# Surface flow: the sum of p2 and q2 as an addition on GpSimd over 128x1024 elements instead of an accumulating DMA

## The chip, the cores and the metric

The kernel runs on one core of a Trainium2 chip. The metric is the device time of one execution in microseconds (us); lower is better. The engines of the core are named as in the profile: PE (TensorE, matmuls), DVE (VectorE), ACT (ScalarE), POOL (GpSimd) and SP (SyncE, which here only issues DMAs). The engines run side by side and meet through semaphores.

## The reference

Four layers in a row over images of shape (4, 16, 512, 512) in fp32: window attention with an MLP, a surface flow of ten time steps, and two residual pairs of 3x3 convolutions. Only the flow matters here:

```python
def step(u, _):
    ux, uy, uxx, uxy, uyy = _derivs(u)          # Sobel 3x3, clipped to +-10
    g2 = ux * ux + uy * uy
    denK = jnp.maximum(1.0 + g2, EPS)
    K = jnp.clip((uxx * uyy - uxy * uxy) / (denK * denK + EPS), -5.0, 5.0)
    denH = jnp.sqrt(1.0 + g2 + EPS)
    H = ((1.0 + uy * uy) * uxx - 2.0 * ux * uy * uxy + (1.0 + ux * ux) * uyy) / (2.0 * denH ** 3 + EPS)
    H = jnp.clip(H, -5.0, 5.0)
    diff = jnp.clip(alpha * K + beta * H, -1.0, 1.0)
    u = u + DT * diff
    u = jnp.pad(u[:, :, 1:-1, 1:-1], ((0, 0), (0, 0), (1, 1), (1, 1)), mode='edge')
    return (u, None)
u, _ = jax.lax.scan(step, x, None, length=TIME_STEPS)      # 10 steps
return 0.7 * u + 0.3 * x
```

The change is about `g2 = ux*ux + uy*uy`, in the kernel's names q2 = p2 + q2.

## The kernel before, in words

The kernel has three stages one after the other: `attention_stage`, `surface_stage` (the flow) and `conv_chain` (both convolution layers). Only `surface_stage` is touched.

It takes the 64 images in 8 groups of 8. A group lies in SBUF as the tensor u with 17 units, each 128 partitions by two images' rows of 512 (128x1024 elements). It goes through its ten time steps there, so there are 8 x 10 x 17 = 1360 units in all. Between two steps SP exchanges halo rows between units by small DMAs, and between two groups it stores u and loads the next group (`boundary`).

Each engine runs a loop of slots written out by hand, and slot n does the work of several units of different age:

- PE (L872) makes five derivatives of unit n in PSUM, in the order B, p, A, q, C, by fp32 matmuls with band matrices: p = ux, q = uy, A, B, C the second derivatives.
- ACT copies them out of PSUM (L895 p, L899 A, L901 q, L909 B, L921 C), squares the clipped p and q together into p2q2 (L929), which is the tile p2 beside the tile q2, and makes the denominators of unit n-2 out of the sum in q2: rK at L913, L915 and L926, rH at L917, L924 and L936, and L904 one slot later. B2 is the square of B (L933).
- DVE clips (L1009 A, L1016 p and q, L1034 C, L1041 B) and makes the products: Ha = (q2 + 1) A (L1038, which reads q2 before the sum overwrites it), nK = -A C (L1027), m = m B (L1031), nK = nK rK of unit n-2 (L1048), rH = beta Hc rH of unit n-2 (L1051), Hc = (p2 + 1) C (L1060), m = -2 p q (L1064), ds (L1021, clipped at L1044), and the edge columns of u (L1056).
- POOL computes nothing. It issues accumulating DMAs (destination = destination + source, SBUF to SBUF) for all sums: nK += B2 (L956, unit n-1), q2 += p2 (L962, unit n), u += ds (L969, three DMAs for unit n-3), Hc += m (L975, unit n-1) and Hc += Ha (L981, unit n).

Every engine takes its instructions in their order, so what stands behind a waiting instruction waits with it. Every tile except u is there twice, by the parity of the unit. `g_sum` is the semaphore of the sum in q2: ACT waits for it ahead of L913, two slots after POOL issues the sum, and POOL waits ahead of L962 for the sum of the unit before. `t1_done` is set by DVE's L1038 and `squared["pq"]` by ACT's L929; POOL waits for both ahead of the sum.

Of the kernel before, what the change touches and what calls it, by code (L numbers as in the profile page):

```python
# [11 lines left out]
ALU = mybir.AluOpType  # L12
# [589 lines left out]
def surface_stage(nc, x1, u10, mats, alpha_in, beta_in, STEPS):  # L602
# [45 lines left out]
    with ExitStack() as ctx:  # L648
# [3 lines left out]
        def sem(name):  # L652
            return ctx.enter_context(nc.semaphore(name))
# [14 lines left out]
        for i, n in enumerate("pq"):  # L668
# [10 lines left out]
        g_sum, ac_done, numk, pq_done, t12_done, numh, u_added = (  # L679
            sem(n) for n in ("g_sum", "ac_done", "numk", "pq_done", "t12_done", "numh", "u_added"))  # L680
        den_squared, den_ln, g_ln, g_pow, pow_ln, rk_done, rh_done = (
            sem(n) for n in ("den_squared", "den_ln", "g_ln", "g_pow", "pow_ln", "rk_done", "rh_done"))
        sums_begun, taps_begun = sem("sums_begun"), sem("taps_begun")
# [4 lines left out]
        def here(unit):  # L688

            return not isinstance(unit, int) or 0 <= unit < TOTAL  # L690

        def wait(eng, s, value):

            if not isinstance(value, int) or value > 0:
                eng.wait_ge(s, value)


        def flat(ap):
            return ap.rearrange("p t w -> p (t w)")

        def buf(n, par):
            return flat(bufs[n][:, par])

        def both(pair, par):

            return pair[:, par].rearrange("p n t w -> p (n t w)")

        def bank(name):

            return banks["pABqC".index(name) % 4]  # L710
# [173 lines left out]
        @block.scalar  # L884
        def _(act):

            act.preload_act_table_set("natural_log_exp_and_others")

            def slot(n, par):

                o = 1 - par
                if here(n):
                    act.wait_ge(made["p"], n + 1)
                    wait(act, pq_done, n - 1)
                    act.activation(buf("pc", par), flat(bank("p")[:, :, :]), ACT.Copy).then_inc(copied["p"], 1)  # L895
                    act.wait_ge(made["A"], n + 1)
                    wait(act, t1_done, n - 1)
                    wait(act, ac_done, n - 1)
                    act.activation(buf("Ac", par), flat(bank("A")[:, :, :]), ACT.Copy).then_inc(copied["A"], 1)  # L899
                    act.wait_ge(made["q"], n + 1)  # L900
                    act.activation(buf("qc", par), flat(bank("q")[:, :, :]), ACT.Copy).then_inc(copied["q"], 1)  # L901
                if here(n - 3):
                    act.wait_ge(pow_ln, n - 2)
                    act.activation(buf("rH", o), buf("rH", o), ACT.Exp, scale=-1.0).then_inc(rh_done, 1)  # L904
                if here(n):
                    act.wait_ge(made["B"], n + 1)
                    wait(act, m_done, n - 1)
                    wait(act, squared["B"], n - 1)
                    act.activation(buf("Bc", par), flat(bank("B")[:, :, :]), ACT.Copy).then_inc(copied["B"], 1)  # L909
                if here(n - 2):  # L910
                    act.wait_ge(g_sum, (n - 1) * 16)
                    wait(act, k_made, n - 3)
                    act.activation(buf("rK", par), buf("q2", par), ACT.Square, bias=1.0).then_inc(den_squared, 1)  # L913
                    act.wait_ge(den_squared, n - 1)
                    act.activation(buf("rK", par), buf("rK", par), ACT.Ln, bias=EPS).then_inc(den_ln, 1)  # L915
                    wait(act, s_done, n - 3)
                    act.activation(buf("rH", par), buf("q2", par), ACT.Ln, bias=1.0 + EPS).then_inc(g_ln, 1)  # L917
                if here(n):
                    act.wait_ge(made["C"], n + 1)
                    wait(act, t2_done, n - 1)  # L920
                    act.activation(buf("Cc", par), flat(bank("C")[:, :, :]), ACT.Copy).then_inc(copied["C"], 1)  # L921
                if here(n - 2):
                    act.wait_ge(g_ln, n - 1)
                    act.activation(buf("rH", par), buf("rH", par), ACT.Exp, scale=1.5).then_inc(g_pow, 1)  # L924
                    act.wait_ge(den_ln, n - 1)
                    act.activation(buf("rK", par), buf("rK", par), ACT.Exp, scale=-1.0).then_inc(rk_done, 1)  # L926
                if here(n):
                    act.wait_ge(clipped["pq"], n + 1)
                    act.activation(both(p2q2, par), both(pq, par), ACT.Square).then_inc(squared["pq"], 1)  # L929
                if here(n - 1):  # L930
                    act.wait_ge(clipped["B"], n)
                    wait(act, k_made, n - 2)
                    act.activation(buf("B2", o), buf("Bc", o), ACT.Square).then_inc(squared["B"], 1)  # L933
                if here(n - 2):
                    act.wait_ge(g_pow, n - 1)
                    act.activation(buf("rH", par), buf("rH", par), ACT.Ln, bias=EPS, scale=2.0).then_inc(pow_ln, 1)  # L936

            for n in range(4):
                slot(n, n % 2)
            with act.Fori(4, TOTAL - 2, 2) as n:  # L940
                slot(n, 0)
                slot(n + 1, 1)
            for n in range(TOTAL - 2, TOTAL + 3):
                slot(n, n % 2)

        @block.gpsimd
        def _(pool):
            def slot(n, par):

                o = 1 - par  # L950
                if here(n - 1):
                    pool.wait_ge(ac_done, n)
                    pool.wait_ge(squared["B"], n)
                    wait(pool, numk, (n - 1) * 16)
                    pool.sem_inc(sums_begun, 1)
                    pool.dma_start(buf("nK", o), buf("B2", o), accum_op=ALU.add).then_inc(numk, 16)  # L956
                if here(n):
                    pool.wait_ge(squared["pq"], n + 1)
                    pool.wait_ge(t1_done, n + 1)
                    wait(pool, g_sum, n * 16)  # L960
                    pool.sem_inc(sums_begun, 1)
                    pool.dma_start(buf("q2", par), buf("p2", par), accum_op=ALU.add).then_inc(g_sum, 16)  # L962
                if here(n - 3):
                    pool.wait_ge(s_clipped, n - 2)
                    wait(pool, u_added, (n - 3) * 48)
                    pool.sem_inc(sums_begun, 1)
                    k, ds = bass.ds((n - 3) % UNITS, 1), bufs["ds"][:, o]
                    for t, rows, found in HALVES:
                        pool.dma_start(u[rows, k, t, 2:W + 2].rearrange("p a w -> p (a w)"), ds[found, t, :], accum_op=ALU.add).then_inc(u_added, 16)  # L969
                if here(n - 1):  # L970
                    pool.wait_ge(t12_done, n * 16)
                    pool.wait_ge(m_done, n)
                    wait(pool, numh, (n - 1) * 16)
                    pool.sem_inc(sums_begun, 1)
                    pool.dma_start(buf("Hc", o), buf("m", o), accum_op=ALU.add).then_inc(numh, 16)  # L975
                if here(n):
                    pool.wait_ge(t1_done, n + 1)
                    pool.wait_ge(t2_done, n + 1)
                    wait(pool, t12_done, n * 16)
                    pool.sem_inc(sums_begun, 1)  # L980
                    pool.dma_start(buf("Hc", par), buf("Ha", par), accum_op=ALU.add).then_inc(t12_done, 16)  # L981

            for n in range(4):
                slot(n, n % 2)
            with pool.Fori(4, TOTAL - 2, 2) as n:
                slot(n, 0)
                slot(n + 1, 1)
            for n in range(TOTAL - 2, TOTAL + 3):
                slot(n, n % 2)
# [441 lines left out]
```

## Time and profile before

| | |
|---|---|
| time, median of 2 runs | 28,650.49 us (28,632.75 to 28,668.22) |
| the profiled execution | 28,647.74 us, its span 28,645.9 us |
| PE busy | 26,744.7 us, 93% |
| DVE busy | 23,740.9 us, 83% |
| ACT busy | 23,103.3 us, 81% |
| POOL busy | 8,975.8 us, 31% |
| TensorE's granted clock, mean | 0.981 |

The span is the time from the first to the last instruction of the profiled execution. The shares are means over three stages with different limits, so they have to be read stage by stage. In the rows below, a row of waits names the engine and instruction that stood still, what released it, the time in all, how often, and the longest. A row of a group has the line, engine and operation, the tiles (out<-in) with their shapes and the count, then busy time and mean duration, then the idle time just before them. "Landing" is the time from the issue of a DMA to its completion.

### The profile page before, as it was taken

How to read it: one execution, taken by the hardware profiler on the slowest of the kernel's cores; microseconds unless marked ns; L12 is line 12 of the kernel's file. 1: busy time of each engine (PE TensorE's matmuls, PEld its weight loads, DVE VectorE, ACT ScalarE, POOL GpSimd, SP SyncE). 2: the span in 40 equal slices, each digit the busy share in tenths (PEclk: the TensorE clock that was granted, in tenths of full speed). 3: DMA queues.
4: the chain of work that ended last, by engine and by line, in shares of the span. 5: the costliest groups of instructions: out<-in, count | busy, mean ns of one | idle time of the engine just before them, and what ended most of it. 6: DMA issues, size and time to landing. Idle time of an engine off the chain costs nothing. (4 is left out here: it accounts for less than half of the span.)

```text
span 28645.9 us, 827717 instructions
## 1 busy us (share of the span) xinstructions
PE 26744.7 (93%) x334232; PEld 12655.2 (44%) x334232; DVE 23740.9 (83%) x26151; ACT 23103.3 (81%) x23277; POOL 8975.8 (31%) x9524
## 2 busy tenths in 40 slices
PE   8999999999989989998999899999989998999799
PEld 5666666444334433443434344334434443444455
DVE  6666666799989989998999899889989998999222
ACT  6666666799989989998999899889989998999111
POOL 0000000244434434443444344434434443444000
PEclk9999999999999999999999999999999999999899
DMA  1111111699999999999999999999999999999654
GB/s 33 32 32 32 32 32 32 126 176 176 178 177 176 177 177 178 176 176 178 176 176 178 178 176 176 180 175 176 176 178 175 176 176 179 176 176 176 119 106 90
DMA packets 1942097, 4147.74 MB, mean 145 GB/s; under 512 B 590960, under 2 KB 722544, under 8 KB 1938160
## 3 DMA queue, kind: packets, MB, share of 16 engines
q0 software_dynamic: 1196800, 3565.77, 70.6%
q1 hardware_dynamic: 701424, 469.69, 8.2%
q10 hardware_dynamic: 41088, 67.14, 1.1%
q8 instruction: 2726, 44.66, 0.6%
q14 instruction: 59, 0.48, 0.0%
HBM read 294.41 MB, written 201.33 MB: 17 GB/s over the span
## 5 line engine op out<-in xcount | busy, mean ns | idle before, releaser
L872 PE MATMUL surf_ps<-surf_u,surf_matf 64*64 64x512 f32 x184960 | 20141.9, 593 | 1129.8 <-ACT surf_pq L895 703.1
L872 PEld LDWEIGHTS surf_ps<-surf_u,surf_matf 64*64 64x64 f32 x184960 | 8316.3, 133 | 12956.2 <-issue 12897.1
L929 ACT ACTIVATE surf_p2q<-surf_pq 128x2048 f32<-128x2048 f32 x1360 | 2599.9, 1912 | 1484.5 <-DVE surf_pq L1016 1484.5
L969 POOL DMA_DIRECT2D surf_u<-surf_ds x4080 | 3458.4, 1156 | 954.0 <-issue 483.3
L962 POOL DMA_DIRECT2D surf_p2q<-surf_p2q x1360 | 1161.3, 854 | 7773.6 <-DVE surf_Ha L1038 7280.0
L956 POOL DMA_DIRECT2D surf_nK<-surf_B x1360 | 1236.4, 909 | 6884.4 <-ACT surf_B L933 6870.3
L1051 DVE SCALAR_TENSOR_TENSOR surf_rH<-surf_Hc,surf_dt_ab,surf_rH 128x1024 f32<-128x1024 f32 x1360 | 1744.0, 1282 | 1454.7 <-DMA surf_Hc<-surf_m 1045.0
L981 POOL DMA_DIRECT2D surf_Hc<-surf_Ha x1360 | 2187.1, 1608 | 351.2 <-DVE surf_Hc L1060 344.2
L975 POOL DMA_DIRECT2D surf_Hc<-surf_m x1360 | 1466.2, 1078 | 1648.1 <-DMA surf_Hc<-surf_Ha 1521.8
L1027 DVE SCALAR_TENSOR_TENSOR surf_nK<-surf_Ac,surf_Cc 128x1024 f32<-128x1024 f32 x1360 | 1666.8, 1226 | 180.6
L1021 DVE SCALAR_TENSOR_TENSOR surf_ds<-surf_nK,surf_dt_ab,surf_rH 128x1024 f32<-128x1024 f32 x1360 | 1731.0, 1273 | 0.3
L1060 DVE SCALAR_TENSOR_TENSOR surf_Hc<-surf_p2q,surf_Cc 128x1024 f32<-128x1024 f32 x1360 | 1666.6, 1225 | 24.0
L404 ACT ACTIVATE att_hid<-att_w,att_b_fc 128x2048 f32<-128x2048 f32 x256 | 503.7, 1968 | 1464.9 <-PE att_w L275 1464.9
L1038 DVE SCALAR_TENSOR_TENSOR surf_Ha<-surf_p2q,surf_Ac 128x1024 f32<-128x1024 f32 x1360 | 1656.0, 1218 | 5.2 <-ACT surf_p2q L929 5.2
L1016 DVE TENSOR_SCALAR surf_pq<-surf_pq 128x2048 f32<-128x2048 f32 x1360 | 1651.9, 1215 | 6.2 <-ACT surf_pq L901 6.2
L1031 DVE TENSOR_TENSOR surf_m<-surf_m,surf_Bc 128x1024 f32<-128x1024 f32 x1360 | 1656.8, 1218 | 0.0
L1064 DVE SCALAR_TENSOR_TENSOR surf_m<-surf_pq 128x1024 f32<-128x1024 f32 x1360 | 1656.7, 1218 | 0.0
L1048 DVE TENSOR_TENSOR surf_nK<-surf_nK,surf_rK 128x1024 f32<-128x1024 f32 x1360 | 1655.2, 1217 | 1.3 <-DMA surf_nK<-surf_B 1.3
L895 ACT ACTIVATE surf_pq<-surf_ps 128x1024 f32<-128x1024 f32 x1360 | 1363.6, 1003 | 331.6 <-PE surf_ps L872 331.6
L483 DVE TENSOR_REDUCE att_mx<-att_w 128x32 f32<-128x2048 f32 x512 | 1173.3, 2292 | 520.8 <-PE att_w L204 520.8
L469 DVE SCALAR_TENSOR_TENSOR att_acc<-att_xin,att_vec,att_acc 128x512 f32<-128x512 f32 x2048 | 1535.1, 750 | 54.3
L901 ACT ACTIVATE surf_pq<-surf_ps 128x1024 f32<-128x1024 f32 x1360 | 1391.3, 1023 | 116.2 <-PE surf_ps L872 98.2
(107 smaller groups left out, 39009.4 us busy)
## 6 DMA issues: line engine op xcount, KB each, us to landing
surf_p2q<-surf_p2q POOLq DMA_DIRECT2D x1360, 512.0 KB, 11.3
surf_Hc<-surf_Ha POOLq DMA_DIRECT2D x1360, 512.0 KB, 13.4
surf_nK<-surf_B POOLq DMA_DIRECT2D x1360, 512.0 KB, 9.6
surf_Hc<-surf_m POOLq DMA_DIRECT2D x1360, 512.0 KB, 11.5
surf_u<-surf_ds POOLq DMA_DIRECT2D x1360, 256.0 KB, 5.7
surf_u<-surf_ds POOLq DMA_DIRECT2D x2720, 128.0 KB, 9.6
att_xin<-in_x SPq DMA_DIRECT2D x2048, 41.2 KB, 2.1
attended<-att_out_rows SPq DMA_DIRECT2D x1024, 64.0 KB, 2.0
```

The source lines that it names most:

```text
L872: mm = pe.matmul(ps[out, t, :], matf[rows, mat, :], u[rows, k, t, off + 2:off + 2 + W], start=(i == 0), stop=(i == len(taps) - 1))
L929: act.activation(both(p2q2, par), both(pq, par), ACT.Square).then_inc(squared["pq"], 1)
L969: pool.dma_start(u[rows, k, t, 2:W + 2].rearrange("p a w -> p (a w)"), ds[found, t, :], accum_op=ALU.add).then_inc(u_added, 16)
L981: pool.dma_start(buf("Hc", par), buf("Ha", par), accum_op=ALU.add).then_inc(t12_done, 16)
L1021: dve.scalar_tensor_tensor(out=buf("ds", o), in0=buf("nK", o), scalar=minus_alpha, in1=buf("rH", o), op0=ALU.mult, op1=ALU.add).then_inc(s ...
L1027: dve.scalar_tensor_tensor(out=buf("nK", o), in0=buf("Ac", o), scalar=-1.0, in1=buf("Cc", o), op0=ALU.mult, op1=ALU.mult).then_inc(ac_done, 1)
L1031: dve.tensor_tensor(buf("m", o), buf("m", o), buf("Bc", o), ALU.mult).then_inc(m_done, 1)
L1038: dve.scalar_tensor_tensor(out=buf("Ha", par), in0=buf("q2", par), scalar=1.0, in1=buf("Ac", par), op0=ALU.add, op1=ALU.mult).then_inc(t1_ ...
L1048: dve.tensor_tensor(buf("nK", par), buf("nK", par), buf("rK", par), ALU.mult).then_inc(k_made, 1)
L1051: dve.scalar_tensor_tensor(out=buf("rH", par), in0=buf("Hc", par), scalar=beta, in1=buf("rH", par), op0=ALU.mult, op1=ALU.mult).then_inc(h ...
L1060: dve.scalar_tensor_tensor(out=buf("Hc", par), in0=buf("p2", par), scalar=1.0, in1=buf("Cc", par), op0=ALU.add, op1=ALU.mult).then_inc(t2_ ...
L1064: dve.scalar_tensor_tensor(out=buf("m", par), in0=buf("pc", par), scalar=-2.0, in1=buf("qc", par), op0=ALU.mult, op1=ALU.mult).then_inc(pq ...
```

## The change

The sum q2 = p2 + q2 of each unit is made by GpSimd itself, as an elementwise addition of two 128x1024 fp32 tiles in SBUF, in the place in POOL's order where it issued the accumulating DMA. POOL's wait on `g_sum` for the sum before and the count `sums_begun` go with the DMA, and ACT's wait on `g_sum` counts by 1 instead of 16. Nothing else changes; the tiles, the other four sums and all other waits stay.

```diff
                 if here(n - 2):
-                    act.wait_ge(g_sum, (n - 1) * 16)
+                    act.wait_ge(g_sum, n - 1)
                     wait(act, k_made, n - 3)
                     act.activation(buf("rK", par), buf("q2", par), ACT.Square, bias=1.0).then_inc(den_squared, 1)
...
                 if here(n):
                     pool.wait_ge(squared["pq"], n + 1)
                     pool.wait_ge(t1_done, n + 1)
-                    wait(pool, g_sum, n * 16)
-                    pool.sem_inc(sums_begun, 1)
-                    pool.dma_start(buf("q2", par), buf("p2", par), accum_op=ALU.add).then_inc(g_sum, 16)
+                    pool.tensor_tensor(buf("q2", par), buf("p2", par), buf("q2", par), ALU.add).then_inc(g_sum, 1)
```

This is POOL's order in the loop of the flow, at the sum of the first of the two slots that the loop holds, with what each row waits for; - is before and + is after the change.

```order
 L695 ISA [waits squared_B,ac_done]
 L956 DMA surf_nK<-surf_B 128x1024 [waits numk]
 L958 REGISTER_ALU
-L695 REGISTER_ALU [waits t1_done,squared_pq]
-L962 DMA surf_p2q<-surf_p2q 128x1024 [waits g_sum]
-L964 REGISTER_ALU
+L960 TENSOR_TENSOR surf_p2q<-surf_p2q 128x1024 [waits t1_done,squared_pq]
+L962 REGISTER_ALU
 L695 ISA [waits s_clipped]
```

The addition stands where the DMA stood, between the sum into nK and the three sums into u; nothing passes anything else. The lines behind it move up by two in the changed kernel (L1038 is L1036 there).

## Rows read from the trace of the kernel before

**Rows 1.** The page, parts 1 and 2: busy time, then tenths in 40 slices.
```profile
PE 26744.7 (93%) x334232; PEld 12655.2 (44%) x334232; DVE 23740.9 (83%) x26151; ACT 23103.3 (81%) x23277; POOL 8975.8 (31%) x9524
...
PE   8999999999989989998999899999989998999799
...
DVE  6666666799989989998999899889989998999222
ACT  6666666799989989998999899889989998999111
POOL 0000000244434434443444344434434443444000
PEclk9999999999999999999999999999999999999899
DMA  1111111699999999999999999999999999999654
```

**Rows 2.** Busy time of each engine in the surface flow; columns in the first line.
```profile
core 0: us, PE busy (x) PEld busy (x) DVE busy (x) ACT busy (x) POOL busy (x), PEclk, DMA share, GB/s
5290.00:26510.00 21220.00, 20113.73 (x184724) 8305.82 (x184720) 19562.92 (x21701) 19235.42 (x19001) 8948.48 (x9493) 0.98 0.98 177
```

**Rows 3.** DMA queues and issues in 6000 to 7000 us: packets, MB, share; KB, landing.
```profile
q0 software_dynamic: 57838, 172.63, 97.7%
...
surf_Hc<-surf_Ha POOLq DMA_DIRECT2D x66, 512.0 KB, 13.3
surf_nK<-surf_B POOLq DMA_DIRECT2D x66, 512.0 KB, 9.5
surf_p2q<-surf_p2q POOLq DMA_DIRECT2D x66, 512.0 KB, 10.6
surf_Hc<-surf_m POOLq DMA_DIRECT2D x66, 512.0 KB, 11.5
surf_u<-surf_ds POOLq DMA_DIRECT2D x66, 256.0 KB, 5.7
surf_u<-surf_ds POOLq DMA_DIRECT2D x132, 128.0 KB, 8.7
```

**Rows 4.** Waits in the surface flow: total us, times, longest.
```profile
ACT surf_p2q L929 <- DVE surf_pq L1016: 1475.0, 1353, 6.2
DVE surf_rH L1051 <- DMA surf_Hc<-surf_m: 1021.4, 495, 11.2
PE surf_ps L872 <- ACT surf_pq L895: 700.8, 418, 5.5
...
DVE surf_rH L1051 <- ACT surf_rH L904: 400.0, 63, 38.2
PE surf_ps L872 <- SPq L841: 368.1, 14, 41.5
...
POOL surf_p2q L962 <- DMA surf_p2q<-surf_p2q: 7.3, 4, 2.0
```

**Rows 5.** Instructions on p2q: ns min/median/max; who waited; landing of the DMA.
```profile
L1038 DVE SCALAR_TENSOR_TENSOR surf_Ha<-surf_p2q,surf_Ac x1360: 1212/1218/1227, 5295.1 to 26540.2; 128x1024 f32<-128x1024 f32 x195
...
L962 POOL DMA_DIRECT2D surf_p2q<-surf_p2q x1360: 850/852/1114, 5297.0 to 26542.0; - x195
...
  ACT surf_rK L913: 8.2, 1
...
DMA to landing us min/median/max: 4.7/11.3/19.1
```

**Rows 6.** The timeline of POOL at the start: its only computing.
```profile
0.25 0.10 POOL L1425 MEMSET const-float32-0.0<- 128x1 f32 x1 [0.25 <-issue]
```

**Rows 7.** The timeline of one slot around L962: start us, us, engine, line.
```profile
12990.66 1.22 DVE L1038 SCALAR_TENSOR_TENSOR surf_Ha<-surf_p2q,surf_Ac 128x1024 f32<-128x1024 f32 x1
...
12991.79 0.69 DVE L1041 TENSOR_SCALAR surf_Bc<-surf_Bc 128x1024 f32<-128x1024 f32 x1
...
12992.40 0.69 DVE L1044 TENSOR_SCALAR surf_ds<-surf_ds 128x1024 f32<-128x1024 f32 x1
...
12992.60 0.85 POOL L962 DMA_DIRECT2D surf_p2q<-surf_p2q  x1 [1.67 <-DVE surf_Ha L1038]
...
12993.00 1.22 DVE L1048 TENSOR_TENSOR surf_nK<-surf_nK,surf_rK 128x1024 f32<-128x1024 f32 x1
...
12994.24 1.29 DVE L1051 SCALAR_TENSOR_TENSOR surf_rH<-surf_Hc,surf_dt_ab,surf_rH 128x1024 f32<-128x1024 f32 x1
```

**Rows 8.** Groups of DVE in the surface flow: busy us, mean ns of one.
```profile
L1031 DVE TENSOR_TENSOR surf_m<-surf_m,surf_Bc 128x1024 f32<-128x1024 f32 x1357 | 1653.1, 1218 | 0.0
...
L1016 DVE TENSOR_SCALAR surf_pq<-surf_pq 128x2048 f32<-128x2048 f32 x1358 | 1649.5, 1215 | 6.2 <-ACT surf_pq L901 6.2
...
L1041 DVE TENSOR_SCALAR surf_Bc<-surf_Bc 128x1024 f32<-128x1024 f32 x1358 | 930.9, 685 | 0.0
```

**Rows 9.** Busy time of each engine around a group boundary, columns as in 2.
```profile
7700.00:8100.00 400.00, 317.17 (x2828) 124.69 (x2824) 300.04 (x334) 295.26 (x292) 141.97 (x146) 0.91 0.93 178
```

## Prediction

> **What bounds the kernel now.** I read the page from the slices down. [rows 1] show three stages: attention to slice 7, the surface flow to slice 37, the convolution chain behind it. Only the flow has GpSimd at work and the DMA engines at 9 tenths; the change is in it alone. It runs from 5290 to 26510 us of the span, 21,220 us for 1360 slots (one unit each), so 15.60 us a slot. The rest, 28,647.7 - 21,220 = 7,428 us, is not touched.
>
> Next the busy times of that stretch [rows 2]: PE 20,114, DVE 19,563, ACT 19,235 and POOL 8,948 us of 21,220; per slot 14.79, 14.38, 14.14 and 6.6 us. Three engines lie within 5% of each other, and the DMA engines are at 0.98 too. Which of them sets the pace is read from the quiet stretch of 1000 us with 66 slots [rows 3]: POOL's queue alone takes 97.7% of 16 engines, 14.8 us a slot. It moves four sums of 512 KB and 512 KB in three parts into u, 2,560 KB a slot. So the DMA engines are the fullest, by a nose.
>
> The waits [rows 4] show how that reaches the others. DVE waits 1,021 us in all at L1051 for the landed sum Hc<-m, in 495 of 1360 slots; ACT in turn waits 1,475 us at L929 for DVE's clip of pq, and PE 701 us for ACT to copy p out of PSUM (L895). PE further waits 368 us for SyncE at L841 (14 times, up to 41.5 us: group boundaries), and DVE 400 us behind ACT L904 at the same places. So DMA -> DVE -> ACT -> PE is the chain of a slow slot, and its head is DVE's wait for DMA.
>
> **The change part by part.**
>
> *The DMA that goes.* 1360 accumulating DMAs of 512 KB each leave POOL's queue: a fifth of 2,560 KB, so 14.8 us a slot becomes about 11.8 us and the DMA engines stop being the bound. The other sums land sooner, and I take DVE's whole wait for them away: -1,021 us of DVE idle time. Its other idle time, 21,220 - 19,563 - 1,021 = 636 us (400 of it at the boundaries), I keep.
>
> *POOL's own time.* The DMA's issue, 0.85 us [rows 5], becomes an addition. POOL is busy 6.6 us a slot, so some 1.3 to 3 us more fits easily in 14 to 17. Behind the addition stand, in POOL's order, the three DMAs into u, Hc<-m, Hc<-Ha and the next nK<-B2. They are issued later by the length of the addition less 0.85 us, but each then finds a queue that is a fifth emptier; I set both at nothing. If that cover is gone, DVE's 1,021 us come back at L1051 and are the price.
>
> *The latency of the sum.* It took 11.3 us to land at the median and 19.1 at most [rows 5]. Its readers (ACT L913 and L917) come two slots, some 31 us, later, and ACT's wait there was 8.2 us once [rows 5]. A sooner sum is worth nothing. The waits on g_sum that go from POOL held it 7.3 us in all [rows 4]: nothing.
>
> *What the addition costs DVE.* This is the term that decides. Before, no row has GpSimd computing on anything but 128x1 constants [rows 6], so it must be bounded. DVE's instructions stand back to back [rows 7]: each starts up to 0.09 us before the one ahead ends, with no free place of a microsecond in the slot. Where GpSimd's addition starts (released by L1038, in the row of the DMA 0.7 us behind its end), DVE is in L1044 and has L1048 and L1051 next. Let x be what DVE loses per addition; the stage is then 19,563 + 636 + 1360x = 20,199 + 1360x, as long as that exceeds PE's floor below.
> - From below x is 0. DVE's L1038 takes 1212 to 1227 ns in all 1360 cases [rows 5], so GpSimd's descriptor work beside it does nothing to it; if an addition is as harmless, DVE loses nothing.
> - From above the nearest thing is the shortest landing of the same sum as a DMA, 4.7 us [rows 5].
> - Between them stand DVE's own rows [rows 8]. A clip of 2048 elements takes 1215 ns and one of 1024 elements 685: 530 ns for 1024 elements and 155 fixed. The two-operand product of 1024 elements (L1031) takes 1218, of which 1063 is streaming. An adder that fetches its operands one after the other streams twice 1063 = 2.13 us.
>
> I take x = 2.13, which is a choice: that GpSimd needs two passes, and that DVE, nearly all of whose instructions move whole tiles in and out of SBUF, stands for that time. No row shows either. It gives 20,199 + 2,897 = 23,096 us, 1,876 more than now. The one-pass row (x = 1.22) would give 21,858, +638; three passes, with the write (x = 3.19), 24,537, +3,317; x = 4.7 26,591, +5,371.
>
> The Trainium skill speaks to just this and against the change. "SBUF — State Buffer", section Who interferes with whom, says that GpSimd reads and writes through a port pair shared with VectorE, and that an instruction of either holds it to its end while the other stands still; it counts VectorE's two-operand instructions and its fast one-operand ones among the holders. "GPSIMD Engine Reference", section 3.1, has 4497 ns for such an addition of 2048 fp32 elements; half of it, an estimate of 2.25 us, would make the stage 23,259 and the run 30,687 us. No run here shows either yet.
>
> **The sum.** 28,648 (the profiled run, 2.7 us under the median of the runs shown) - 1,021 + 2,897 = 30,524 us, +6.5%. PE then has 17.0 us for 14.8 us of work. Its clock stays, I think: at the boundary stretch, with PE busy 317 of 400 us, the granted clock was still 0.91 [rows 9], while at 23,096 us PE would be busy 87%; even at 0.91 against 0.98 its 14.8 us become 15.9, under 17.0.
>
> **The rivals.**
> 1. *The addition is free for DVE (x below about 0.3).* For it: L1038's constant duration. Against it: it rests on descriptor work, not on an operation that reads operands of 512 KB. Then PE sets the pace: 20,114 of work and its other idle time, 1,106 - 701 = 405, make 20,519 us, and the run 27,947, -2.4%. If only some of PE's 701 us goes (ACT is at 14.14 us a slot, and the slots need not be even) it is 28,100 to 28,300, within 2%.
> 2. *A part of it is hidden (x from 0.3 to 1.17).* DVE breaks even at x = 1,021/1360 = 0.75 us, and is 2% slower (573 us) at 1.17. For it: DVE's remaining idle time of 0.47 us a slot can take some. Against it: that time is bunched at boundaries, and even one pass of DVE's own speed is above 1.17. About 28,650.
> 3. *GpSimd waits for DVE instead.* Since DVE has hardly a gap, the addition may begin only where DVE stops. Then Hc<-m behind it is issued late, and DVE's next idle time is L1051 itself, for the addition and then a landing of 11.5 us [rows 3]: some 14 us a slot at worst, or anything between. Against it: a boundary between two instructions of DVE comes every 1.3 us at the latest [rows 7]. From 32,000 up, and 2.5 us of such waiting a slot is where it would pass the likeliest case.
>
> **How the numbers follow.** Likeliest, 0.70: DVE stands for one to three passes, 29,286 (28,648 + 638) to 31,965 us, and 30,524 at two. Rival 1: 0.18, of which 0.12 below -2% and 0.06 within. Rival 2: 0.08, within 2%. Rival 3: 0.04, slower. So faster 0.12, within 2% (about what a measurement of this kernel can tell from no change) 0.14, slower 0.74. The range goes from 28,050, which leaves out the faster case (0.12), to 31,970, which leaves out rival 3: 0.16 left out. The likeliest case's own range is 29,290 to 31,970.
>
> **What would show it.** Right: POOL rows of the addition near 2.1 to 2.3 us; DVE rows behind L1038 (L1044, L1048 or L1051 by the old numbers) longer by about its length, or a gap before them; DVE's share of the flow near all of it, its wait for Hc<-m gone or small; DMA share of the flow near 0.72; PE's wait for L895's copy grown to about 2 us a slot. Wrong, if DVE's busy time in the flow stays at 19,563 us and PE's at the front (rival 1), or if the addition's row is preceded by long idle time and DVE waits longer for Hc<-m than now (rival 3). The step I trust least is x.

## The result, and the profile after

| | before | after |
|---|---|---|
| time, median | 28,650.49 us | 30,076.41 us (30,062.19 to 30,090.63) |
| ratio, 95% interval | | 1.0501 (1.0482 to 1.0519) |
| span of the profiled execution | 28,645.9 us | 30,060.4 us |
| DVE busy | 23,740.9 us | 26,642.0 us |
| PE busy | 26,744.7 us | 26,783.1 us |
| POOL busy | 8,975.8 us | 11,256.3 us |
| granted clock | 0.981 | 0.993 |

The changed kernel is 5% slower, 1,426 us. The line numbers behind the change are lower by two: L1042, L1046, L1049 and L1058 were L1044, L1048, L1051 and L1060.

The slices of the page show the exchange; they answer to [rows 1].

```profile
PE   8999999888888888888888888888888888888799
...
DVE  6666666999999999999999999999999999999422
...
PEclk9999999999999999999999999999999999999899
DMA  1111111677777787778777777777787777777654
```

DVE has gone from 9 tenths with dips to 9 in every slice of the flow, the DMA engines from 9 to 7 or 8 tenths. The busy times of the flow, from the same start to where the changed one ends, answer to [rows 2]:

```profile
core 0: us, PE busy (x) PEld busy (x) DVE busy (x) ACT busy (x) POOL busy (x), PEclk, DMA share, GB/s
5290.00:27930.00 22640.00, 20145.20 (x184552) 8215.77 (x184548) 22437.80 (x21679) 19190.99 (x18979) 11213.06 (x9481) 1.00 0.73 134
```

DVE is busy 22,438 of 22,640 us, so 202 us idle where it was 1,657. The DMA share fell from 0.98 to 0.73. The queues and issues of 1000 quiet us, now with 60 slots in them, answer to [rows 3] (packets, MB and share of 16 engines; then KB and the median time to landing):

```profile
q0 software_dynamic: 44096, 125.59, 69.5%
...
surf_Hc<-surf_m POOLq DMA_DIRECT2D x60, 512.0 KB, 6.2
surf_Hc<-surf_Ha POOLq DMA_DIRECT2D x60, 512.0 KB, 7.9
```

The sum Hc<-m lands after 6.2 us instead of 11.5. The waits of the flow, in all us, times and longest, answer to [rows 4]:

```profile
ACT surf_p2q L929 <- DVE surf_pq L1014: 3375.8, 1354, 3.0
PE surf_ps L872 <- ACT surf_pq L895: 2466.4, 1335, 2.3
...
DVE surf_rH L1049 <- ACT surf_rH L904: 6.0, 5, 2.4
...
DVE surf_rH L1049 <- DMA surf_Hc<-surf_m: 0.3, 1, 0.3
```

DVE's wait for the landed sum, 1,021 us before, is 0.3 us. ACT's wait for DVE has more than doubled (1,475 before) and PE's for ACT has grown from 701 to 2,466 us: the chain is now DVE -> ACT -> PE, and DVE waits for next to nothing. Where its time goes is in the timeline of one slot, answering to [rows 7] (start us, duration us):

```profile
12992.85 1.22 DVE L1036 SCALAR_TENSOR_TENSOR surf_Ha<-surf_p2q,surf_Ac 128x1024 f32<-128x1024 f32 x1
...
12993.99 0.69 DVE L1039 TENSOR_SCALAR surf_Bc<-surf_Bc 128x1024 f32<-128x1024 f32 x1
...
12994.23 2.67 POOL L960 TENSOR_TENSOR surf_p2q<-surf_p2q 128x1024 f32<-128x1024 f32 x1 [1.17 <-DVE surf_Ha L1036]
...
12994.59 2.85 DVE L1042 TENSOR_SCALAR surf_ds<-surf_ds 128x1024 f32<-128x1024 f32 x1
...
12997.37 1.21 DVE L1046 TENSOR_TENSOR surf_nK<-surf_nK,surf_rK 128x1024 f32<-128x1024 f32 x1
...
12998.27 1.72 POOL L967 DMA_DIRECT2D surf_u<-surf_ds  x2 [1.37 <-DVE surf_ds L1042]
```

GpSimd starts its addition at 12994.23, while DVE's clip L1039 runs. That clip ends on time. The next one, L1042, is 0.69 us of work and takes 2.85: it ends 0.54 us after the addition. The addition ends at 12996.90. The groups of DVE in the flow show that this holds for the mean of all slots (busy us, mean ns of one), answering to [rows 8]:

```profile
L1042 DVE TENSOR_SCALAR surf_ds<-surf_ds 128x1024 f32<-128x1024 f32 x1353 | 3876.3, 2865 | 0.0
...
L1029 DVE TENSOR_TENSOR surf_m<-surf_m,surf_Bc 128x1024 f32<-128x1024 f32 x1355 | 1650.5, 1218 | 0.0
...
L1039 DVE TENSOR_SCALAR surf_Bc<-surf_Bc 128x1024 f32<-128x1024 f32 x1356 | 928.8, 685 | 0.0
```

The clip of ds takes 2,865 ns in the mean. In [rows 7] it was 0.69 us, and its twin L1039 still is 685. The others kept their length to within 20 ns; only the small operation on the edge columns of u, L1054, went from 182 to 229 ns. The shortest, median and longest duration of the instructions on p2q, answering to [rows 5], show that the loss isn't bound to the clip:

```profile
L1036 DVE SCALAR_TENSOR_TENSOR surf_Ha<-surf_p2q,surf_Ac x1360: 1214/1217/1226, 5297.5 to 27981.9; 128x1024 f32<-128x1024 f32 x195
L960 POOL TENSOR_TENSOR surf_p2q<-surf_p2q x1360: 2372/2672/2689, 5298.9 to 27983.2; 128x1024 f32<-128x1024 f32 x195
L1058 DVE SCALAR_TENSOR_TENSOR surf_Hc<-surf_p2q,surf_Cc x1360: 1224/1225/4080, 5299.2 to 27988.9; 128x1024 f32<-128x1024 f32 x195
```

L1036, ahead of the addition, is untouched in all 1360 cases. The Hc product L1058, an instruction with two operands, reached 4,080 ns: in the first slots no unit n-3 exists, L1042 is not there to be hit, and L1058 (twice) and L1046 (once) were hit in its place.

### The profile page after: what moved, and what is told of

Its sections match the earlier page's. It is cut to its first block and busy times, and to the rows that moved or that the text cites. A ratio compares the mean times of both kernels' runs of the same rounds, so it can differ in the third digit from the quotient of the medians.

```text
span 30060.4 us, 825006 instructions
## 1 busy us (share of the span) xinstructions
PE 26783.1 (89%) x334232; PEld 12568.7 (42%) x334232; DVE 26642.0 (89%) x26151; ACT 23081.5 (77%) x23277; POOL 11256.3 (37%) x9524
## 5 line engine op out<-in xcount | busy, mean ns | idle before, releaser
L960 POOL TENSOR_TENSOR surf_p2q<-surf_p2q 128x1024 f32<-128x1024 f32 x1360 | 3627.2, 2667 | 6815.5 <-DVE surf_Ha L1036 6815.2
L1042 DVE TENSOR_SCALAR surf_ds<-surf_ds 128x1024 f32<-128x1024 f32 x1360 | 3889.8, 2860 | 0.1
L973 POOL DMA_DIRECT2D surf_Hc<-surf_m x1360 | 2158.9, 1587 | 15.9 <-DMA surf_Hc<-surf_Ha 4.0
L979 POOL DMA_DIRECT2D surf_Hc<-surf_Ha x1360 | 1785.2, 1313 | 12.5 <-issue 7.6
L1049 DVE SCALAR_TENSOR_TENSOR surf_rH<-surf_Hc,surf_dt_ab,surf_rH 128x1024 f32<-128x1024 f32 x1360 | 1730.1, 1272 | 13.2 <-DMA surf_Hc<-surf_m 7.2
L1058 DVE SCALAR_TENSOR_TENSOR surf_Hc<-surf_p2q,surf_Cc 128x1024 f32<-128x1024 f32 x1360 | 1671.4, 1229 | 1.4
L1036 DVE SCALAR_TENSOR_TENSOR surf_Ha<-surf_p2q,surf_Ac 128x1024 f32<-128x1024 f32 x1360 | 1655.6, 1217 | 5.2 <-ACT surf_p2q L929 5.2
L1029 DVE TENSOR_TENSOR surf_m<-surf_m,surf_Bc 128x1024 f32<-128x1024 f32 x1360 | 1656.6, 1218 | 0.0
L1062 DVE SCALAR_TENSOR_TENSOR surf_m<-surf_pq 128x1024 f32<-128x1024 f32 x1360 | 1656.5, 1218 | 0.0
L1046 DVE TENSOR_TENSOR surf_nK<-surf_nK,surf_rK 128x1024 f32<-128x1024 f32 x1360 | 1649.9, 1213 | 5.4 <-DMA surf_nK<-surf_B 5.4
L915 ACT ACTIVATE surf_rK<-surf_rK 128x1024 f32<-128x1024 f32 x1360 | 1438.5, 1058 | 43.2
```

The source lines that it names most:

```text
L960: pool.tensor_tensor(buf("q2", par), buf("p2", par), buf("q2", par), ALU.add).then_inc(g_sum, 1)
L1029: dve.tensor_tensor(buf("m", o), buf("m", o), buf("Bc", o), ALU.mult).then_inc(m_done, 1)
L1042: dve.tensor_scalar(buf("ds", o), buf("ds", o), DT, -DT, ALU.min, ALU.max).then_inc(s_clipped, 1)
L1049: dve.scalar_tensor_tensor(out=buf("rH", par), in0=buf("Hc", par), scalar=beta, in1=buf("rH", par), op0=ALU.mult, op1=ALU.mult).then_inc(h ...
L1058: dve.scalar_tensor_tensor(out=buf("Hc", par), in0=buf("p2", par), scalar=1.0, in1=buf("Cc", par), op0=ALU.add, op1=ALU.mult).then_inc(t2_ ...
```

## Experiments

Theory S: GpSimd's addition stands DVE still for as long as it streams its operands, and that is all of the loss. Rivals: the loss comes from POOL's order (O), from both costs adding (A), or from something that depends on the place of the addition.

### What the DMA's removal is worth alone

```diff
-                    pool.tensor_tensor(buf("q2", par), buf("p2", par), buf("q2", par), ALU.add).then_inc(g_sum, 1)
+                    pool.sem_inc(g_sum, 1)
```

> Leaves the sum out: neither a DMA nor an addition, so q2 keeps the square of q. It measures what the removed DMA is worth alone. Theory S (GpSimd's addition stands DVE still, 2.17 us a slot, and nothing else costs): DVE's wait of 1021 us for the landed Hc<-m is gone and PE sets the pace, 27,950 us, or 27,600 if the boundary waits of 368 us go as well. Rival O (the loss comes from POOL's order, from issues that come at another time without the DMA): no better than before, 28,650 or above.

Measured: 27,518.0 us, 0.9610 of before (0.9594 to 0.9626). Rival O in its first form falls: POOL's order without the DMA costs nothing. What a long instruction in that order costs, by the later issues behind it, this run does not test; the changed kernel's waits show it, with DVE 0.3 us behind Hc<-m. The quiet 1000 us show the new leader (columns as above):

```profile
6000.00:7000.00 1000.00, 1000.00 (x9324) 505.39 (x9320) 988.67 (x1096) 977.94 (x960) 385.10 (x410) 1.00 0.81 147
```

PE is busy all of it at 9324 matmuls, at 136 a slot 14.59 us a slot. I had expected 27,950, or 27,600 with the boundary waits gone. They are not quite gone: PE still waited 214 us for SP at the boundaries. Against this kernel, and not against the one before, the addition on GpSimd costs 30,076 - 27,518 = 2,558 us, 1.88 us a slot. So the removal brought 1,120 us (28,638 in the same session less 27,518) and the addition took 2,558.

### The addition on DVE itself

```diff
                     dve.tensor_scalar(buf("Bc", par), buf("Bc", par), *CLIP).then_inc(clipped["B"], 1)
+                    dve.wait_ge(t1_done, n + 1)
+                    dve.tensor_tensor(buf("q2", par), buf("p2", par), buf("q2", par), ALU.add).then_inc(g_sum, 1)
...
-                    pool.tensor_tensor(buf("q2", par), buf("p2", par), buf("q2", par), ALU.add).then_inc(g_sum, 1)
```

> The same addition on DVE, behind its clip of B, with no DMA and nothing on POOL. Theory S: it costs DVE its own 1.13 us (1.22 less the overlap with its neighbours) instead of 2.17, so 1,040 ns x 1360 = 1,410 us less than with GpSimd: about 28,650 us, the time of the kernel before. Rival O (the loss comes through POOL's longer queue, later sums into u and Hc): the same gain over the GpSimd version, but DVE idle and not 99% busy. Rival T (DVE stands still whenever its two-operand work meets POOL's descriptor work): slower than 28,900.

Measured: 28,746.3 us, 1.0040 (1.0026 to 1.0054): 0.4% slower than before, about 100 us more than expected, and 1,330 us faster than with the addition on GpSimd. The groups of DVE in the flow:

```profile
L1037 DVE TENSOR_TENSOR surf_p2q<-surf_p2q 128x1024 f32<-128x1024 f32 x1360 | 1660.0, 1221 | 0.0
...
L1040 DVE TENSOR_SCALAR surf_ds<-surf_ds 128x1024 f32<-128x1024 f32 x1360 | 936.9, 689 | 0.1
```

The addition takes DVE 1,221 ns, and the clip of ds (L1040 here) is back at 689. DVE's busy time over the whole kernel is 25,181.8 us, 1,441 more than before, 1.06 us a slot; with GpSimd it was 2,901 more. DVE pays twice as much for having the addition made elsewhere as for making it. Rival O falls: DVE is 99% busy here as well (990 of 1000 us in the quiet stretch), so it is DVE's load that sets both times. Rival T, that DVE's two-operand work stands still beside POOL's descriptor work (above 28,900 us), falls too: L1044 and L1047, the products that were L1048 and L1051, take 1,221 and 1,282 ns as before.

### DMA and addition together

The kernel before, with one addition more on tiles that nobody reads.

```diff
                     pool.dma_start(buf("q2", par), buf("p2", par), accum_op=ALU.add).then_inc(g_sum, 16)
+                    wait(pool, spare_done, n)
+                    pool.tensor_tensor(spare[:, 0], spare[:, 1], spare[:, 2], ALU.add).then_inc(spare_done, 1)
```

> The kernel before, its DMA kept, plus an addition of two spare tiles of the same size on GpSimd behind the issue of the DMA, whose result nobody reads. Theory S: DVE's 19,563 us + 1360 x 2.17 = 22,514 us with its idle time hidden, about 30,100 us if the boundary idle time is hidden by the slower pace, about 30,450 if only a relieved DMA queue hides it. Rival A (the two costs add, since waits and standstill lie in different places): 28,650 + 2,950 = 31,600 us.

Measured: 30,587.7 us, 1.0687 (1.0670 to 1.0705). Rival A (31,600) falls: most of the wait for DMA is hidden behind the standstill. The groups of DVE (the lines are nine higher than in the changed kernel):

```profile
L1058 DVE SCALAR_TENSOR_TENSOR surf_rH<-surf_Hc,surf_dt_ab,surf_rH 128x1024 f32<-128x1024 f32 x1359 | 3762.3, 2768 | 482.1 <-ACT surf_rH L906 271.9 <-DMA surf_Hc<-surf_m 209.7
L1055 DVE TENSOR_TENSOR surf_nK<-surf_nK,surf_rK 128x1024 f32<-128x1024 f32 x1360 | 2519.0, 1852 | 1.5 <-DMA surf_nK<-surf_B 1.5
...
L1051 DVE TENSOR_SCALAR surf_ds<-surf_ds 128x1024 f32<-128x1024 f32 x1359 | 936.3, 689 | 0.0
```

Here the addition starts later, behind the DMA's issue, and meets other instructions: L1058 (before: L1051) at 2,768 instead of 1,282 ns, L1055 at 1,852 instead of 1,217, together 2.12 us a slot, while the clip of ds stays at 689. The operands are tiles that no other engine touches once DVE has set them to zero at the start, so it isn't p2 or q2 that is fought over. The run is 511 us slower than the changed kernel. Its waits say why:

```profile
PE surf_ps L874 <- SPq L843: 291.9, 9, 42.7
...
DVE surf_rH L1058 <- ACT surf_rH L906: 271.9, 9, 40.6
...
DVE surf_rH L1058 <- DMA surf_Hc<-surf_m: 216.3, 85, 6.6
```

292 us of PE and 272 of DVE behind ACT are at group boundaries, where SP loads the next images, and 216 us are for Hc<-m. At nearly the same pace of 16.7 to 16.9 us a slot the changed kernel has 0 from SP, 6 and 0.3 us. So at this pace it is the emptier DMA queue that took the boundary waits away. The pace has a share in it too. With the full queue PE waited 368 us for SP at 15.15 us a slot and 292 here; with the sum's DMA gone it waited 214 us at 14.59 us a slot (no sum), 105 at 15.6 (addition on DVE) and 0 in the changed kernel. Neither alone took them away; both together did. I had kept them in my sum.

### Half the addition

```diff
-                    pool.tensor_tensor(buf("q2", par), buf("p2", par), buf("q2", par), ALU.add).then_inc(g_sum, 1)
+                    pool.tensor_tensor(buf("q2", par)[:, 0:512], buf("p2", par)[:, 0:512], buf("q2", par)[:, 0:512], ALU.add).then_inc(g_sum, 1)
```

> The changed kernel with GpSimd adding only 512 of the 1024 columns; the other half of the sum is left out. If DVE stands still for the streaming of the operands, its loss falls from 2.17 us by about half to 1.1 us: the flow is 14.38 + 1.1 = 15.5 us a slot, 28,700 us in all. If the loss is mainly a fixed cost of taking and giving back whatever the two engines share, it stays near 2 us and the run near 29,900.

Measured: 28,707.4 us, 1.0021 (1.0011 to 1.0031), against 28,700 expected from the first theory and 29,900 from the fixed cost. The clip of ds, then the addition on POOL:

```profile
L1042 DVE TENSOR_SCALAR surf_ds<-surf_ds 128x1024 f32<-128x1024 f32 x1360 | 2409.4, 1772 | 0.1
```

```profile
L960 POOL TENSOR_TENSOR surf_p2q<-surf_p2q 128x512 f32<-128x512 f32 x1360 | 2143.4, 1576 | 6815.2 <-DVE surf_Ha L1036 6814.9
```

The clip loses 1,772 - 685 = 1,087 ns, half of 2,180. The addition is 1,576 ns for 512 columns and 2,667 for 1024: 1,091 for 512 columns and 485 that do not depend on the size. So DVE loses about the streaming alone. The other 0.49 us costs nothing: it is about the 0.45 us in which DVE finishes the instruction that it is in (L1039) and GpSimd waits.

### One operand, and none

```diff
-                    pool.tensor_tensor(buf("q2", par), buf("p2", par), buf("q2", par), ALU.add).then_inc(g_sum, 1)
+                    pool.sem_inc(sums_begun, 1)
+                    pool.tensor_copy(buf("q2", par), buf("p2", par)).then_inc(g_sum, 1)
```

> GpSimd copies p2 over q2 (128x1024, one operand) instead of adding; the sum is left out. Two-pass theory (the operands are fetched one after another and DVE stands for each): one pass, DVE loses about 1.06 us a slot, 28,650 us. Rival (the write or the instruction's fixed part is what holds DVE): more than 1.6 us, above 29,300. Rival (only a two-operand instruction of GpSimd holds DVE): no loss, near the 27,518 us of the kernel without the sum.

Measured: 28,372.7 us, 0.9906 (0.9886 to 0.9926). One slot:

```profile
13000.61 0.68 DVE L1040 TENSOR_SCALAR surf_Bc<-surf_Bc 128x1024 f32<-128x1024 f32 x1
...
13000.85 1.34 POOL L961 COPY surf_p2q<-surf_p2q 128x1024 f32<-128x1024 f32 x1 [1.11 <-DVE surf_Ha L1037]
...
13001.22 1.53 DVE L1043 TENSOR_SCALAR surf_ds<-surf_ds 128x1024 f32<-128x1024 f32 x1
```

With `pool.memset(buf("q2", par), 1.0)` in its place:

> GpSimd writes ones over q2 (128x1024, no operand read) instead of adding; the sum is left out. If only GpSimd's reading stands DVE still: no loss, near 27,518 us, and DVE's clip behind the release (L1044 of the kernel before) stays at 685 ns. If the writing does it too, that clip, which is a fast one-operand instruction, is longer by what is left of the memset when the instruction ahead ends, 0.5 to 1 us, and the run is 27,900 to 28,500. A two-operand instruction of DVE should then not be longer, by the Trainium skill's page SBUF — State Buffer, section Who interferes with whom.

Measured: 28,359.2 us, 0.9901 (0.9881 to 0.9921). One slot:

```profile
12997.57 0.69 DVE L1040 TENSOR_SCALAR surf_Bc<-surf_Bc 128x1024 f32<-128x1024 f32 x1
...
12997.80 1.35 POOL L961 MEMSET surf_p2q<- 128x1024 f32 x1 [1.10 <-DVE surf_Ha L1037]
...
12998.17 1.52 DVE L1043 TENSOR_SCALAR surf_ds<-surf_ds 128x1024 f32<-128x1024 f32 x1
```

Copy and memset cost the same: the clip is 1.53 and 1.52 us, 0.84 more than its 0.69, and both GpSimd instructions take about 1.35. The writing does stand the fast clip still; the theory that only GpSimd's reading matters falls here. So does the pass of 1.06 us: one operand costs 0.85 us, two cost 2.18, not twice 0.85. The loss follows what GpSimd itself needs, not a pass at DVE's rate.

### The same two, beside other instructions of DVE

```diff
                     pool.wait_ge(t1_done, n + 1)
+                    if here(n - 3):
+                        pool.wait_ge(s_clipped, n - 2)
```

This holds GpSimd until the clip of ds is done, and so starts it beside L1048, with L1051 behind it, both with two operands from SBUF (their lines are higher by one where the memset is). First with the memset:

> GpSimd's memset of q2 (no sum) as in the run before, but released later, by DVE's clip of ds of unit n-3, so that it lies beside DVE's two-operand product and scale (L1048 and L1051 of the kernel before) instead of beside the fast one-operand clip, which it made 0.83 us longer at 28,359 us. If it is the class of DVE's instruction that decides (a write-only instruction of GpSimd meets only the fast one-operand ones, as the Trainium skill's page SBUF — State Buffer has it in Who interferes with whom), DVE loses nothing and the run is 27,500 to 27,650 us. If any GpSimd instruction stands any DVE instruction still, the loss stays 0.8 to 1.3 us a slot: 28,350 to 29,000.

Measured: 27,523.7 us, 0.9610 (0.9590 to 0.9629), the time without any sum on POOL (27,518.0). The groups of DVE, then POOL's memset:

```profile
L1052 DVE SCALAR_TENSOR_TENSOR surf_rH<-surf_Hc,surf_dt_ab,surf_rH 128x1024 f32<-128x1024 f32 x1360 | 1747.0, 1285 | 312.2 <-ACT surf_rH L904 278.0 <-DMA surf_Hc<-surf_m 33.2
...
L1049 DVE TENSOR_TENSOR surf_nK<-surf_nK,surf_rK 128x1024 f32<-128x1024 f32 x1360 | 1656.0, 1218 | 1.1 <-DMA surf_nK<-surf_B 1.1
...
L1045 DVE TENSOR_SCALAR surf_ds<-surf_ds 128x1024 f32<-128x1024 f32 x1360 | 933.7, 687 | 0.1
```

```profile
L963 POOL MEMSET surf_p2q<- 128x1024 f32 x1360 | 1296.5, 953 | 8501.3 <-DVE surf_Ha L1039 5299.5 <-DVE surf_ds L1045 3201.8
```

Nothing is longer: 1,285, 1,218 and 687 ns. The memset too is short now, 953 ns instead of 1,347 with the clip's rest ahead of it. One slot shows where it lies:

```profile
10995.90 1.22 DVE L1049 TENSOR_TENSOR surf_nK<-surf_nK,surf_rK 128x1024 f32<-128x1024 f32 x1
...
10996.14 0.95 POOL L963 MEMSET surf_p2q<- 128x1024 f32 x1 [2.31 <-DVE surf_ds L1045]
```

It begins and ends while L1049 runs, so it is L1049 that it met, and hardly L1052 (from 10997.11 on). A write-only instruction of GpSimd and this two-operand instruction of DVE ran side by side, and neither was longer; a release some 1.2 us later made 836 us of difference. By the Trainium skill, page "SBUF — State Buffer", section Who interferes with whom, a DVE instruction with two SBUF inputs contends with a GpSimd instruction that reads SBUF and not with one that only writes. The runs agree: 0 for the memset here, 2.08 us a slot for the addition in the next run.

Then with the addition, complete:

> The changed kernel's addition, complete, released later in the same way, beside the two-operand L1048 and L1051. If a reading GpSimd instruction stands every kind of DVE instruction here still for its streaming time, the loss only moves from the clip to L1051: 2.17 us, or up to 2.4 where no rest of an instruction covers its start, so 30,080 to 30,400 us. If the place matters (POOL's later sums into u, or a victim that DVE can do without), it differs by more than 400 us either way.

Measured: 30,004.8 us, 1.0474 (1.0457 to 1.0492). One slot:

```profile
12990.32 1.22 DVE L1048 TENSOR_TENSOR surf_nK<-surf_nK,surf_rK 128x1024 f32<-128x1024 f32 x1
...
12990.49 3.28 POOL L962 TENSOR_TENSOR surf_p2q<-surf_p2q 128x1024 f32<-128x1024 f32 x1 [2.24 <-DVE surf_ds L1044]
...
12991.46 3.39 DVE L1051 SCALAR_TENSOR_TENSOR surf_rH<-surf_Hc,surf_dt_ab,surf_rH 128x1024 f32<-128x1024 f32 x1
```

The addition is issued to GpSimd at 12990.49 and takes 3.28 us, since it first waits for the end of L1048 (12991.54); then L1051 waits for it and takes 3.39 instead of 1.28. Over the run L1051's mean is 3,365 ns, 2.08 more than before. For the addition, which reads, the class of its victim changes almost nothing. Each of the two waits for the one that began first. The run came out 75 us under the lower end of what I expected: I had set at least 2.17 us, and the 0.09 us that are missing are 120 us over 1360 slots.

### A part on DVE, the rest by DMA

If DVE has a little room and the DMA queue leads, a part of the sum can move.

```diff
+                    dve.wait_ge(t1_done, n + 1)
+                    dve.tensor_tensor(buf("q2", par)[:, 0:256], buf("p2", par)[:, 0:256], buf("q2", par)[:, 0:256], ALU.add).then_inc(g_part, 1)
...
-                    pool.dma_start(buf("q2", par), buf("p2", par), accum_op=ALU.add).then_inc(g_sum, 16)
+                    pool.dma_start(buf("q2", par)[:, 256:], buf("p2", par)[:, 256:], accum_op=ALU.add).then_inc(g_sum, 16)
```

> A quarter of the sum (256 of 1024 columns) as an addition on DVE behind its clip of B, three quarters as the DMA as before; the result is complete. Theory S: DVE 14.38 + 0.33 = 14.7 us a slot, the DMA queue 14.8 - 0.74 = 14.1, PE 14.8 as before, so PE leads and most of its 701 us of waiting goes: 27,950 to 28,300 us. Rival L (DVE's wait for Hc<-m is latency behind a busy queue and not its load, so a twentieth less load changes nothing): 28,650 to 28,900.

Measured: 28,154.6 us, 0.9834 (0.9818 to 0.9850): faster than both kernels by more than the intervals, by 1.7% against the one before. The part of the sum on DVE, then the quiet 1000 us, then the waits:

```profile
L1045 DVE TENSOR_TENSOR surf_p2q<-surf_p2q 128x256 f32<-128x256 f32 x1360 | 571.6, 420 | 0.0
```

```profile
6000.00:7000.00 1000.00, 998.31 (x9164) 407.91 (x9160) 990.26 (x1147) 952.95 (x944) 439.72 (x474) 1.00 0.97 171
```

```profile
PE surf_ps L873 <- SPq L842: 323.3, 14, 37.9
...
DVE surf_rH L1055 <- DMA surf_Hc<-surf_m: 268.4, 109, 9.6
...
PE surf_ps L873 <- ACT surf_pq L896: 156.0, 85, 5.2
```

256 columns cost DVE 420 ns. PE is at 998 of 1000 us with 9164 matmuls, 14.84 us a slot where it was 15.15 (66 slots in [rows 3]). DVE's wait for Hc<-m fell from 1,021 to 268 us and PE's for ACT from 701 to 156. Rival L falls. With 384 columns:

> 384 of the 1024 columns of the sum on DVE, 640 by DMA; the result is complete. With 256 columns DVE was 99% busy in the quiet stretch at 14.84 us a slot, and the boundaries kept 323 us of PE's time. With 384, DVE takes 0.13 us a slot more, +180 us, and the DMA queue 0.37 us less, which shortens the boundaries by some 50 to 100 us: 28,150 to 28,300 us, no better than with 256. If the DMA queue still leads with 256 columns, it is faster instead, 27,950.

Measured: 28,346.1 us, 0.9898 (0.9882 to 0.9915): slower than with 256, slightly above what I expected. PE is at 983 of 1000 us, its wait for ACT is 396 us where it was 156, and DVE is at 990: DVE leads again. Its part of the sum takes 550 ns, the 0.13 us more that I had expected. The clip of ds behind it is longer as well: its mean is 795 ns, where it was 689 with 256 columns, and 0.11 us a slot are 144 us in all. POOL's issue of the DMA (L964) runs beside it and takes 1.17 us at the median instead of the 0.85 of [rows 5]. So a clip and the issue of a DMA can hold each other up a little; whether this is the same standstill as the addition's was not tested. Of the two shares 256 is the better; no other was tried.

## Why the prediction was right, and where its sizes were off

Forecast 30,524 us, range 28,050 to 31,970, slower; measured 30,076 us. The way and the mechanism held, and the steps were these.

- **The DMA engines stop being the bound.** Right. I put the queue at 11.8 us a slot; it is 695 / 60 = 11.6. DVE's 1,021 us of waiting went whole.
- **The idle time that I kept.** Of DVE's idle time I kept 636 us, 400 of them at the boundaries; 202 us are left. This is 434 of the 456 us by which the stage was forecast too long (23,096 against 22,640 us); the other 22 are in DVE's busy time. The step that was off is "Its other idle time ... I keep": I took the boundary waits for a matter of SP and the images. They hung on the same DMA queue and on the pace together: the run with DMA and addition has most of them again at nearly the same pace, and the run without the sum, with the emptier queue at a faster pace, has a part of them.
- **x, what DVE loses per addition.** I took 2.13 us from between 0 and 4.7; the clip of ds lost 2.18 (2,865 - 685), the run with the late addition 2.08, the one with DMA and addition 2.12. The value was right and its derivation was not: the copy shows 0.85 us for one operand, not 1.06. The doubling of DVE's pass hit 2.18 by luck. What is shown is that x is GpSimd's own streaming time and that half the columns halve it. The row for one pass in my sum was uneven besides: it took a whole instruction of DVE, 1.22 us, where two and three passes were built from the 1.06 of streaming; at 1.06 one pass would have lain inside rival 2.
- **Where the addition starts.** I took the place from the DMA's row, 0.7 us behind L1038. The addition starts 0.16 us behind it (L1036, which ends at 12994.07), beside the clip of B, and so its victim is the clip of ds. The late addition shows that this hardly matters for x: 2.08 against 2.18 us.
- **GpSimd's 2.25 us from the Trainium skill.** "GPSIMD Engine Reference", section 3.1, has 4497 ns for 2048 elements. Here 1024 elements took 2,372 ns at the least and 2,672 at the median, with what it waits for DVE in it. Near enough for a sum; the estimate taken as x would have made 30,687 us.
- **POOL's later issues and the sooner sum cost nothing.** Right. Behind the addition Hc<-m is issued later, and DVE still waits only 0.3 us for it. POOL's wait for DVE's clip ahead of the sums into u, 1,836 us in all, is a result of the standstill, and nobody waits behind it.
- **PE's clock.** Right: granted 0.993 over the span, with PE 89% busy.
- **Rival 1 (free for DVE).** It fell at the clip's 2,865 ns. Its argument, L1038's constant length, was weak from the start: in [rows 7] POOL stood idle from 12990.93 on, waiting for this very instruction, so there was hardly any descriptor work beside it. I had priced the rival at 27,947, and the run without the sum made 27,518, for two reasons: part of the boundary waits goes as well, and PE's matmuls themselves took less (26,488 us busy instead of 26,745; why is open). So a free addition would have been worth 4%, not 2.4%.
- **Rival 2 (a part is hidden, x up to 1.17).** It fell at x = 2.18 us and a run 5% slower.
- **Rival 3 (GpSimd waits for DVE instead).** It fell: GpSimd gets in at the next end of a DVE instruction, 0.45 us (beside the clip) or 1.05 us (beside the product) later.

The balance: 1,021 us of waiting for Hc<-m and 434 of other idle time went, 1,455 in all, and DVE's busy time in the flow grew by 2,875. That makes the stage 1,420 us longer; the two profiled spans differ by 1,414.5. The durations add up to a little more: the clip L1042 alone grew by 2,948 us and the other groups together by 10, but some 84 us more of them overlap with a neighbour, and busy time counts an overlap once.

## What to carry to other kernels

Before moving elementwise work to a GpSimd that stands idle, add its streaming time to DVE's load and see whether DVE has that much idle time in the same stage; here it had 1.2 us a slot, most of it a result of the queue, against 2.2. Price the same work on DVE too: here it was half as dear for DVE when DVE made it itself (1.06 against 2.18 us). And when a queue leads by a nose, try moving a part of one transfer before the whole of it: a quarter won 1.7% here, where the whole move lost 5% on GpSimd and 0.4% on DVE.

## What the runs showed of the hardware that I had not expected

- A GpSimd memset of 128x1024 beside a two-operand instruction of DVE cost DVE nothing (27,524 us) and beside a fast one-operand clip 0.83 us a slot (28,359 us). The same instruction, some 1.2 us later, changed the time by 3%.
- Duration rows of GpSimd contain the wait for DVE: the same addition is 2,372 ns at its shortest, 2,667 in the mean beside a clip and 3,227 beside a two-operand product; the same memset 953 and 1,347.
- The standstill is paid by the DVE instruction behind the one that runs when GpSimd starts, and shows as its busy time. DVE's busy share of 89% therefore looks like work.
- A DMA queue at 98% had made the group boundaries longer too. PE's wait for SP's loads was 368 us with it and 214 us without the sum's DMA (share 0.81), at a slightly faster pace; it was 0 only in the changed kernel, with a share of 0.73 and 16.7 us a slot.
